# Gated cross-attention block: when the projections load their constants, how they store the last image key, and where the remainder tokens stand

## The reference, cut to what matters

```python
n = layernorm(x)
q     = rms_norm(n @ w_q.T + b_q, g_q)                  # 8 x 512 x 512
k_img = rms_norm(ctx[:, :257] @ w_k_img.T + b_k_img, g_k_img)
v_img = ctx[:, :257] @ w_v_img.T + b_v_img
k     = rms_norm(ctx[:, 257:] @ w_k.T + b_k, g_k)
v     = ctx[:, 257:] @ w_v.T + b_v
out   = attention(q, k_img, v_img) + attention(q, k, v, mask=arange(1344) < lens)
x = x + tanh(g_xattn) * (out @ w_o.T + b_o)
y = ternary_linear(gelu(ternary_linear(layernorm(x), W1, b1)), W2, b2)
return x + tanh(g_ffn) * quantize_4bit(y)
```

## Time and profile before

| | us |
|---|---|
| median of 3 runs | 3497.87 (3493.28 to 3501.6) |
| time of the profiled execution | 3523.74 |
| its span | 3521.9 |
| PE busy | 3159.8 (90%) |
| DVE busy | 2123.4 (60%) |
| ACT busy | 1568.4 (45%) |
| POOL busy | 1321.9 (38%) |

### The profile page before, as it was taken

One profiled execution on the slowest core, in us unless ns is written; L12 is line 12 of the kernel. 1 busy time (PEld: TensorE's weight loads), 2 busy tenths in 40 slices (PEclk: granted clock), 3 DMA queues, 4 the chain that ended last, 5 costly groups with the idle time before them and its releaser, 6 DMA issues. The chain is left out here.

```text
span 3521.9 us, 50452 instructions
## 1 busy us (share of the span) xinstructions
PE 3159.8 (90%) x16268; PEld 1914.0 (54%) x16268; DVE 2123.4 (60%) x3591; ACT 1568.4 (45%) x2973; POOL 1321.9 (38%) x483
## 2 busy tenths in 40 slices
PE   6999999996799999999999999999993288999992
PEld 5777777775444444444444444444430166777771
DVE  4666667663666666666666666666643876343435
ACT  3334344332255565665555555655562144222222
POOL 0000000000268667676676676766763053000000
PEclk8999999998699999999999999999996599999996
DMA  5777777779642433424434344243302063000005
GB/s 145 163 167 162 167 162 165 163 159 118 129 92 59 102 76 78 102 55 99 89 64 102 70 84 101 52 102 84 70 16 101 12 189 105 1 1 0 0 0 191
DMA packets 359474, 334.40 MB, mean 95 GB/s; under 512 B 40112, under 2 KB 290032, under 8 KB 358776
## 3 DMA queue, kind: packets, MB, share of 16 engines
q1 hardware_dynamic: 355080, 323.61, 41.1%
q10 hardware_dynamic: 4224, 8.39, 0.6%
HBM read 210.77 MB, written 121.15 MB: 94 GB/s over the span
## 5 line engine op out<-in xcount | busy, mean ns | idle before, releaser
L895 ACT ACTIVATE at_probs<-at_st 128x512 f32<-128x512 f32 (+1 forms) x1664 | 913.9, 595 | 710.7 <-PE at_st L752 697.8
L925 DVE TENSOR_REDUCE at_cm<-at_mx 128x2 f32<-128x896 f32 x768 | 821.1, 1091 | 613.5 <-PE at_mx L768 613.5
L724 POOL TENSOR_TENSOR at_added<-at_added,at_probs 128x2048 f32<-128x2048 f32 x192 | 879.2, 4579 | 79.9 <-ACT at_probs L895 70.9
L768 PE MATMUL at_mx<-at_kst,at_qst 97*128 97x448 f32 (+1 forms) x2048 | 648.1, 385 | 56.9 <-DMA at_kst<-stack_rows 33.6
L768 PEld LDWEIGHTS at_mx<-at_kst,at_qst 97*128 97x128 f32 x2048 | 382.5, 193 | 507.0 <-issue 242.0
L752 PE MATMUL at_st<-at_qst,at_kst 101*128 101x512 f32 (+1 forms) x1664 | 622.9, 436 | 14.1 <-ACT at_probs L895 10.9
L790 PE MATMUL at_acc<-at_probs,at_vt 128*32 128x512 f32 (+2 forms) x3584 | 478.4, 608 | 0.9 <-ACT at_probs L895 0.9
L752 PEld LDWEIGHTS at_st<-at_qst,at_kst 101*128 101x128 f32 (+1 forms) x1664 | 297.0, 186 | 306.8 <-ACT at_probs L895 287.7
L692 POOL MEMSET at_ones<- 128x32 f32 x1 | 0.1, 129 | 842.4 <-POOLq L262 842.4
L724 POOL TENSOR_TENSOR at_added<-at_probs 128x2048 f32<-128x2048 f32 x32 | 146.1, 4566 | 410.0 <-ACT at_probs L895 410.0
L1370 ACT ACTIVATE ff_h<-ff_psa,ff_b1c,alpha 128x512 f32<-128x512 f32 x128 | 99.3, 777 | 344.3 <-PE ff_psa L1347 344.3
(11 more groups left out here) (201 smaller groups left out, 4682.9 us busy)
## 6 DMA issues: line engine op xcount, KB each, us to landing
at_kst<-k_high SPq DMA_DIRECT2D x256, 200.1 KB
at_kst<-k_low SPq DMA_DIRECT2D x128, 200.1 KB
pj_xin<-in_ctx_dram SPq DMA_DIRECT2D x96, 256.0 KB, 4.6
k_high<-pj_kh SPq DMA_DIRECT2D x96, 256.0 KB, 3.5
k_low<-pj_kl SPq DMA_DIRECT2D x96, 256.0 KB, 5.2
values<-pj_vs SPq DMA_DIRECT2D x96, 256.0 KB, 5.0
at_vt<-values SPq DMA_DIRECT2D x32, 768.0 KB
at_qst<-q_high SPq DMA_DIRECT2D x64, 256.0 KB, 4.6
```

The costliest lines, as they stand in the source:

```text
L724: pool.tensor_tensor(added[:], so_far, probs[:, SLOT[t]], ALU.add).then_inc(S["add_done"], 1)
L768: pe.matmul(mx[:, bank, 0:kn], qst[w.j][0:MROWS, h, qt * P:(qt + 1) * P], kst[w.j][0:MROWS, h, k0:k0 + kn], start=True, stop=True).then_in ...
L895: act.activation(probs[0:kn, SLOT[t], h, :], st[0:kn, h % 2, :], ACT.Exp, scale=SCALE).then_inc(S["exp_done"], 1)
L925: dve.tensor_reduce(dst, mx[:, 2 * slot:2 * slot + 2, 0:kn], AX.X, ALU.max, negate=last).then_inc(S["mx_free"], 1)
```

## The change

1. The first three inputs and the eight constants are issued by SP in `prepare_weights`, behind the five weights. Their buffers and semaphores move to a class `Started`, made before that stage.
2. On DVE the tokens begin at once. The tables of live rows are made behind the step of token 0 (`which_live`), the mask row behind that of token 10 (`masks`); SP stores the mask at token 12.
3. The `extra` token's keys go to two small arrays `k_last_high` and `k_last_low` of [4, 128, 8], by one DMA each. `load_stack` reads each group's column from them by three DMAs of 32 x 4 single elements, and reads 1600 instead of 1601 keys by the others; PE's wait for `q_in` counts the three as well.
4. The list of tokens is `ORDER`: batches 0 to 6, then `extra` and three `rem`, then batch 7, then the last `rem`. The loop holds batches 1 to 5; the rest is written out. Counts for semaphores come from tables.

The diff, cut to its core:

```diff
@@ prepare_weights
             for w, src in enumerate(sources):
                 sp.dma_start(nat[w][:], src.rearrange("(o p) i -> p o i", p=P)).then_inc(loaded[w], 16)
+            if started:
+                started.load(sp)
+class Started:
...
+    def load(self, sp):
+        for n, (_, kind, idx) in enumerate(ORDER[:AHEAD]):
+            k0 = idx * P if kind == "img" else NIMG + idx * P
+            sp.dma_start(self.xin[n][:], self.ctx_in[0, k0:k0 + P, :]).then_inc(self.x_ready[n], 16)
+        for t in ("img", "txt", "q"):
+            sp.dma_start(self.bias[t][:], self.rows["b_" + t].partition_broadcast(P)).then_inc(self.const_in, 16)
+            sp.dma_start(self.gain[t][:], self.rows["g_" + t].partition_broadcast(P)).then_inc(self.const_in, 16)
+        sp.dma_start(self.len_i[:], self.lens.partition_broadcast(P)).then_inc(self.const_in, 16)
+        sp.dma_start(self.klen_i[:], self.lens.rearrange("(b o) -> b o", o=1), allow_slow_non_contiguous=True).then_inc(self.const_in, 16)
@@ the list of tokens
-ENDING = [("extra", 0)] + [("rem", k) for k in range(4)]
+BETWEEN = [("extra", 0), ("rem", 0), ("rem", 1), ("rem", 2)]
+ORDER = [(i, kind, idx) for i in range(B - 1) for kind, idx in SEQ]
+ORDER += [(None, kind, idx) for kind, idx in BETWEEN]
+ORDER += [(B - 1, kind, idx) for kind, idx in SEQ] + [(None, "rem", 3)]
@@ tokens
-    with repeat(nc, eng, 1, B - 1) as i:
+    with repeat(nc, eng, 1, B - 2) as i:
         for k in range(NSEQ):
             step(Token(i, k))
-    for k in range(NSEQ):
-        step(Token(B - 1, k))
-    for k in range(len(ENDING)):
-        step(Token(B, k))
+    for n in range(NSEQ * (B - 2), len(ORDER)):
+        step(Token(0, n))
@@ store, on SP
                 if kind == "extra":
-                    for c in range(NG):
-                        out_k(khv[:, :, c, SK - 1].rearrange("b d -> d b").bitcast(F32), h3[:, c, 0:B], allow_slow_non_contiguous=True)
-                        out_k(klv[:, :, c, SK - 1].rearrange("b d -> d b").bitcast(F32), l3[:, c, 0:B], allow_slow_non_contiguous=True)
+                    out_k(kxh_d.rearrange("c d b -> d c b").bitcast(F32), h3[:, :, 0:B])
+                    out_k(kxl_d.rearrange("c d b -> d c b").bitcast(F32), l3[:, :, 0:B])
@@ SP's stream in project
+            for n in range(len(ORDER)):
+                step(Token(0, n))
+                if n == AUX_AT:
+                    sp.wait_ge(S["aux_set"], 6)
+                    for r in range(2):
+                        sp.dma_start(aux_d.rearrange("(b r) s k -> r b s k", r=2)[r], aux[:]).then_inc(S["aux_out"], 16)
+            store(Token(0, len(ORDER) - 1))
@@ DVE's stream in project
+            def step_with_tables(t):
+                step(t)
+                if early(t.n, 1):
+                    which_live()
+                if early(t.n, AUX_AT) and t.n == AUX_AT - 2:
+                    masks()
+            dve.wait_ge(const_in, 16 * 8)
+            dve.wait_ge(S["idx_set"], 1)
+            tokens(nc, dve, step_with_tables)
@@ load_stack, in attend
+                for r, d in enumerate((kxh_d, kxh_d, kxl_d)):
+                    sp.dma_start(kst[p][r * HD:(r + 1) * HD, :, SK - 1:SK].bitcast(F32),
+                                 d[G % NG, :, G // NG:G // NG + 1].bitcast(F32).rearrange("(h d) b -> d h b", d=HD),
+                                 allow_slow_non_contiguous=True).then_inc(q_in[p], 16)
                 for h in range(HG):
                     for r, d in enumerate((kh_d, kh_d, kl_d)):
-                        sp.dma_start(kst[p][r * HD:(r + 1) * HD, h, 0:SK].bitcast(F32),
-                                     d[G, h * HD:(h + 1) * HD, :].bitcast(F32)).then_inc(k_in[p][h], 16)
+                        sp.dma_start(kst[p][r * HD:(r + 1) * HD, h, 0:SK - 1].bitcast(F32),
+                                     d[G, h * HD:(h + 1) * HD, 0:SK - 1].bitcast(F32)).then_inc(k_in[p][h], 16)
@@ maxima, on PE
-                    pe.wait_ge(q_in[w.j], 48 * (w.i + 1))
+                    pe.wait_ge(q_in[w.j], 96 * (w.i + 1))
```

More of the change, by code:

```diff
@@ L43 @@
 AUX = 5
+AHEAD = 3
 class Names:
@@ L125, in _, with __init__ @@
                                   ALU.subtract).then_inc(low_done, 1)
+class Started:
+    def __init__(self, nc, ctx, ctx_in, lens, rows):
+        a = Names(nc, ctx, "pj")
+        self.ctx_in, self.lens, self.rows = ctx_in, lens, rows
+        self.xin = [a.sb(f"xin{p}", [P, D]) for p in range(4)]
+        self.bias = {k: a.sb(f"bias_{k}", [P, D]) for k in ("img", "txt", "q")}
+        self.gain = {k: a.sb(f"gain_{k}", [P, D]) for k in ("img", "txt", "q")}
+        self.len_i = a.sb("len_i", [P, B], I32)
+        self.klen_i = a.sb("klen_i", [B, 1], I32)
+        self.x_ready = [a.sem(f"x_ready{p}") for p in range(4)]
+        self.const_in = a.sem("const_in")
+    def load(self, sp):
[7 more added lines that the diff above has]
+        sp.dma_start(self.klen_i[:], self.lens.rearrange("(b o) -> b o", o=1), allow_slow_non_contiguous=True).then_inc(self.const_in, 16)
 class Seg:
@@ L205 @@
+V_STORES = {"q": 0, "rem": 2}
 class Token:
     def __init__(self, i, k):
-        if k >= NSEQ and not (isinstance(i, int) and i == B):
+        known = isinstance(i, int)
+        if not known and k < 0:
+            i, k = i - 1, k + NSEQ
+        elif not known and k >= NSEQ:
             i, k = i + 1, k - NSEQ
-        if k < 0:
-            i, k = i - 1, k + NSEQ
-        self.i, self.k = i, k
-        self.tail = isinstance(i, int) and i == B
-        self.real = not self.tail or k < len(ENDING)
+        self.n = NSEQ * i + k
+        self.real = not known or 0 <= self.n < len(ORDER)
@@ L216, in __init__ @@
         if not self.real:
             return
[L218 to L233 removed]
+        self.k, self.p, self.x4 = k, k % 2, k % 4
@@ new lines, in __init__ @@
+        if known:
+            self.i, self.kind, self.idx = ORDER[self.n]
+            earlier = ORDER[:self.n]
+            self.vn = sum(kind != "q" for _, kind, _ in earlier)
+            self.vp = self.vn % 2
+            values = [kind for _, kind, _ in ORDER if kind != "q"]
+            ready = sum(LOADS.get(kind, 1) for n, (_, kind, _) in enumerate(ORDER[:self.n + 1]) if n % 4 == self.x4)
+            self.x_ready = 16 * ready
+            self.k_before = 16 * sum(K_STORES.get(kind, 2) for n, (_, kind, _) in enumerate(earlier) if n % 2 == self.p)
+            self.v_before = 16 * sum(V_STORES.get(kind, 1) for n, kind in enumerate(values[:self.vn]) if n % 2 == self.vp)
+            self.k_stored = self.k_before + 16 * K_STORES.get(self.kind, 2)
+            self.v_stored = self.v_before + 16 * V_STORES.get(self.kind, 1)
+            return
@@ L235, in at @@
+        self.i = i
+        self.kind, self.idx = SEQ[k]
+        vk = sum(kind != "q" for kind, _ in SEQ[:k])
+        self.vn, self.vp = NVAL * i + vk, vk % 2
+        self.x_ready = 16 * ((NSEQ // 4) * i + k // 4 + 1)
+        self.k_before = 32 * ((NSEQ // 2) * i + k // 2)
+        self.v_before = 16 * ((NVAL // 2) * i + vk // 2)
     def at(self, step):
+        if isinstance(self.n, int):
+            return Token(0, self.n + step)
         return Token(self.i, self.k + step)
@@ L263, in project @@
         a = Names(nc, ctx, "pj")
-        xin = [a.sb(f"xin{p}", [P, D]) for p in range(4)]
+        xin, bias, gain, len_i, klen_i = started.xin, started.bias, started.gain, started.len_i, started.klen_i
         xh = [a.sb(f"xh{p}", [P, D], F32R) for p in range(2)]
@@ L275, in project @@
         stats = [a.sb(f"stats{p}", [P, 6]) for p in range(2)]
-        bias = {k: a.sb(f"bias_{k}", [P, D]) for k in ("img", "txt", "q")}
-        gain = {k: a.sb(f"gain_{k}", [P, D]) for k in ("img", "txt", "q")}
         one = a.sb("one", [P, 1])
-        len_i = a.sb("len_i", [P, B], I32)
         len_f = a.sb("len_f", [P, B])
@@ L358, in step @@
                     store(t.at(-1))
[L360 to L372 removed]
+            for n in range(len(ORDER)):
[5 more added lines that the diff above has]
+            store(Token(0, len(ORDER) - 1))
             sp.wait_ge(S["aux_out"], 32)
[L374 to L375 removed]
+            for n in (-2, -1):
+                t = Token(0, len(ORDER) + n)
                 sp.wait_ge(k_saved[t.p], t.k_stored)
```

95 lines of the change are left out of this document (35 added, 60 removed).

## The result

The changed kernel takes 3488.76 us (median of 22 runs, 3484.71 to 3503.84); the kernel before took 3497.18 us beside it (22 runs, 3493.28 to 3509.8). The ratio is 0.9979, 95% interval 0.9969 to 0.9989: some 7 to 8 us faster, where 26.6 were forecast. The time lies outside the forecast range.

A forecast was written before the change was run, and what follows sets the result against it. TensorE was taken as almost always busy mid-projections and in attention, so only the projections' two ends and the stall before the second could give time; terms summed to -26.6 us, from median 3497.87 to 3471.3 us, range 3462 to 3486 us.

The forecast's parts named there:

- Part 1: Start of projections: inputs and constants issued behind the weights; first product 12.8 us earlier, DVE's first low part released by ACT.
- Part 2: First batch of projections: live-row tables made later cost +0.6 us; mask computed and stored there, mostly covered, +1.0 us together.
- Part 3: Extra token near the projections' end: two compact key stores replace eight element stores and remove a stall, -6.3 us.
- drain: Last bias addition to attention's first load: less ACT waiting and fewer stores, -11.6 us; sign: 14 to 16 us, not 26.1.
- Part 4: Projections' end: three remainders ahead of the last batch delay its queries, +1.5 us (0 to 4); end gains -11.6 us.
- Part 5: Start of attention: three extra column loads per group stand between queries and keys, +1.0 us (0.5 to 3).
- (a): Rival, last batch: the remainders' backlog only moves, all 6.3 us reappear there, drain gains 9.4 us; 3478.3 us, chance 0.12.
- (b): Rival, before projections: constants share bandwidth with weights, so projections begin up to 8.3 us later; 3479.6 us, chance 0.06.
- (c): Rival, attention's start: three small loads paid one after the other, 6 us instead of 1; 3476.3 us, chance 0.05.
- (d): Rival, attention: small loads bind each group and make the kernel slower by over 0.2%; 3505 us, chance 0.02.
- (e): Rival, unrolled last two batches: savings at both ends come back as longer DMA waits, no gain; 3494 us, chance 0.03.

The follow-up runs named there:

- key_by_elements: Changed kernel with the extra token's keys again sent by eight stores of single elements and attention loading key tiles whole; ratio 1.0009 [0.9998, 1.002] against the kernel before.
- before_again: The kernel before, unchanged, run for a second trace on the same chip as the changed kernel; ratio 1.0004 [0.9993, 1.0014] to the kernel before.
- after_again: The changed kernel, unchanged, run for a second trace on the same chip as the kernel before; ratio 0.9977 [0.9965, 0.9988] to the kernel before.

## Why the prediction was wrong

Each term of the sum, from the traces of the runs above:

| | forecast | shown |
|---|---|---|
| Part 1, start | -12.8 | -12.4 (first product: mean 42.5 us in eight traces of the kernel before and its shifts, 30.2 in eleven with Part 1; first bias addition: 47.8 and 35.1) |
| Part 2, live tables | +0.6 | +1.7 (step 0: 9.8 for 8.1) |
| Part 2, mask computed and stored in batch 0 | +1.0 | +8.9 (computed: step 10 +1.7, of which steps 11 to 13 give back 0.8; stored: step 14 +8.0) |
| Part 3, stall | -6.3 | -5.8 (mean of the same eight, 5.0 to 6.5; 6.6 in `key_by_elements`) |
| drain, 25.8 to 16.5 us (means of eight and nine traces) | -11.6 | -9.3: mask gone 5.1, order 3.4, the last 0.8 not separated |
| Part 4, middle | +1.5 | -2 to +3 |
| Part 5, start of attention | +1.0 | +0.4 |
| place of xh and xl | none | +4 to +6 |
| batch 6, now unrolled | none | +0.7 (96.5 us for 95.8, in the traces with fast products); no run has its cause |
| sum | -26.6 | about -10 |

The terms are uncertain by 2 or 3 us together with the scatter of single traces, and the measured 7 to 8 us agree with the sum within that.

**The step that failed most** is the second half of Part 2. I wrote that "the transfer engines have about a quarter free, so most of both is covered". The free quarter is a mean over 500 us. Behind the mask's two transfers half of the engines' time was free from 120 to 130 us (shares of 0.52 and 0.54), and still an input came 6.0 us late for PE: free time in the mean did not help the transfer that was needed. I had priced the very same two stores at 4.1 us of the drain, at the end, and should have asked for the same there: who needs an engine in those microseconds? The mask's computation was covered by half: its 1.7 us stand in step 10, and the next three steps give back 0.8. The tables' 1.7 us stand whole in step 0.

**The step that was missing**: nothing in the text asked what the new class does to the addresses. The sum took PE's pace, and the 6.38 us of the earlier trace rows, as given. A list of what the change moves has to hold the buffers too.

**The drain was sized 2 us too well.** Part 4 let ACT's wait for old values go for 5.3 us (10.8 to 5.4 us from the last bias addition to the end of the last low part, so that held) and left 9.0 us from there to attention's first load: 1.5 until data flow, 6.5 for them, 1 for the receipt. That stretch is 10.0 us in the first trace and 10.8 to 11.7 us in the other eight. No row shows the 1.5 and the 1 us by themselves.

**What held**: Part 1 within half a microsecond on average, with its sign (released by ACT); the stall of Part 3 to 0.5 us; most of the drain, though the 14 to 16 us named as its sign were met by the first trace alone (15.4, and 16.5 on average). In Part 5 the three loads cost 0.4 us and not three fixed costs one after the other. The section quoted there has its 2 us for transfers that GpSimd issues, while SP issues these, so the run is no test of that figure. The rivals (a), (b), (c) and (d) did not come true: the middle cost at most 3 us, PE's work on the weights ends 0.4 us later on average (23.7 for 23.3 us), the three loads cost 0.4 us, and attention's pace is the same. Of (e), batch 6 and the middle together hold at most 4 us.

**Carrying over to the median.** "Nothing in the change depends on what separates the two" held for the terms. But the two first traces differ by 38.4 us where the medians differ by 8.4; read alone, they would have spoken for an even larger gain than a forecast that was 18 us off.

## What to carry to other kernels

Moving work to where "there is room" needs the room at that moment and on those engines, not in the mean: look who needs an input in the next microseconds, and send a large transfer of few rows in pieces. A change of allocation order is a change of its own: compare the addresses of the operands of the hot loop, and try a pad before judging the rest. And take the trace of both kernels more than once, on one chip, before differences of a few microseconds are read from them.

## What the runs showed of the hardware

- The place in SBUF of a product's left operand against its right one changed PE's pace by 1.4% (6.38 to 6.47 us for a token with 24 products), with all operands on multiples of 64 bytes.
- Behind two transfers of 250 KB with 8 rows PE waited 6.0 us for an input when SP issued them and 5.0 us when POOL did; behind ten of 50 KB, one a token, it did not wait.
- Beside a 4.84 us instruction of POOL, one of DVE took 4.49 us, where it takes 0.55 us with POOL idle (seen once).
- The end of attention, from its thirtieth store of results to the next stage's first load, takes 67 to 70 us in nine of the twenty traces and 76 to 79 us in eleven, in both kernels. The granted clock tells them apart. The mean clock of the whole run goes with it: 0.949 or 0.950 with the long end and 0.954 with the short one in the kernel before and its pads, 0.951 to 0.953 and 0.954 to 0.958 in the changed kernel and its variants. Stretches of `before_again` (length, PE busy, clock, DMA share, GB/s):

```profile
2620.00:2640.00 20.00, 18.20 (x98) 1.00 0.00 1
2640.00:2650.00 10.00, 8.30 (x35) 0.93 0.01 2
2650.00:2660.00 10.00, 9.26 (x38) 0.50 0.07 26
2660.00:2670.00 10.00, 9.02 (x40) 0.50 0.00 0
```

and of `after_again`, 6 us earlier in its course:

```profile
2640.00:2650.00 10.00, 8.29 (x58) 1.00 0.08 28
2650.00:2660.00 10.00, 2.75 (x24) 0.79 0.00 0
```

In the first, PE falls to its lower level, 1.2 GHz, with some 18 us of work left, after it had been busy for 18.20 us of 20 and 8.30 of 10. What decides it was not tried. The 9 us are as large as the effect under study, and as the distance between the two groups of runs above.
